# Softmax denominators by additions in SBUF, and fewer, larger stack DMAs

## The reference, cut to what matters

```python
Q = x @ W_Q.T; K = x @ W_K.T; V = x @ W_V.T          # 16 heads of 32
attn = einsum('bhqd,bhkd->bhqk', Q, K) * scale        # causal: keys after the query are masked
probs = softmax(attn, axis=-1)
y = einsum('bhqk,bhkd->bhqd', probs, V) @ W_O.T
x = layernorm(x + y)
x = layernorm(x + ffn(x))                             # top-1 of 8 experts, weighted
```

## Time and profile before

| | |
|---|---|
| median of 3 runs | 2947.55 us (2947.26 to 2957.64) |
| profiled execution, span from first to last instruction | 2947.9 us |
| TensorE, VectorE, ScalarE, GpSimd busy | 90%, 53%, 36%, 22% |

### The profile page before, as it was taken

One profiled execution on the slowest core, in us unless ns is written; L12 is line 12 of the kernel. 1 busy time (PEld: TensorE's weight loads), 2 busy tenths in 40 slices (PEclk: granted clock), 3 DMA queues, 4 the chain that ended last, 5 costly groups with the idle time before them and its releaser, 6 DMA issues. The chain is left out here.

```text
span 2947.9 us, 51268 instructions
## 1 busy us (share of the span) xinstructions
PE 2664.0 (90%) x16384; PEld 1627.8 (55%) x16385; DVE 1563.5 (53%) x2843; ACT 1065.4 (36%) x2153; POOL 660.7 (22%) x1022
## 2 busy tenths in 40 slices
PE   3999989998999999998999899989999999438886
PEld 2654665457554755475546654565447554436665
DVE  2566446645564456535663466445644564365554
ACT  2245314541445134522453145414541345132332
POOL 2111221113121311122112211131213110235544
PEclk9999999999999999999999999999999999669999
DMA  8422142314331433124221422152314320163332
GB/s 284 115 73 98 39 142 70 90 58 127 90 101 48 118 102 97 50 79 129 74 93 51 139 71 80 58 144 73 101 51 122 87 80 8 43 208 119 121 123 82
DMA packets 131006, 282.95 MB, mean 96 GB/s; under 512 B 33026, under 2 KB 42242, under 8 KB 128452
## 3 DMA queue, kind: packets, MB, share of 16 engines
q1 hardware_dynamic: 100920, 208.62, 23.7%
q0 software_dynamic: 28304, 70.64, 7.8%
q10 hardware_dynamic: 1536, 0.53, 0.1%
HBM read 133.04 MB, written 47.53 MB: 61 GB/s over the span
## 5 line engine op out<-in xcount | busy, mean ns | idle before, releaser
L638 ACT ACTIVATE probs<-score 128x512 f32<-128x512 f32 (+3 forms) x1536 | 690.2, 489 | 812.3 <-PE score L944 511.3
L695 DVE TENSOR_REDUCE tile_max<-maxp 128x1 f32<-128x512 f32 (+3 forms) x1072 | 679.7, 659 | 513.2 <-PE maxp L929 347.6
L940 PE MATMUL score<-q_stack,k_stack 97*128 97x512 f32 (+2 forms) x1536 | 548.5, 410 | 17.6 <-ACT probs L638 16.3
L880 PE MATMUL proj<-xt,w_qk 128*128 128x512 f32 x1536 | 458.8, 413 | 61.5 <-DMA w_qk<-w_qk_parts 49.8
L924 PE MATMUL maxp<-k_stack,q_stack 96*128 96x512 f32 (+2 forms) x1360 | 466.5, 397 | 16.2 <-DVE tile_max L695 12.5
L924 PEld LDWEIGHTS maxp<-k_stack,q_stack 96*128 96x128 f32 x1360 | 240.5, 193 | 312.3 <-issue 225.7
L940 PEld LDWEIGHTS score<-q_stack,k_stack 97*128 97x128 f32 x1536 | 290.3, 194 | 195.0 <-ACT probs L638 178.6
L880 PEld LDWEIGHTS proj<-xt,w_qk 128*128 128x128 f32 x1536 | 280.9, 193 | 118.5 <-DMA w_qk<-w_qk_parts 49.5
L962 PE MATMUL y_ps<-probs,v 128*32 128x512 f32 (+3 forms) x3072 | 327.5, 498 | 8.8 <-DVE rows L719 7.8
L962 PE MATMUL den_ps<-probs,ones_f 128*32 128x512 f32 (+3 forms) x3072 | 326.5, 497 | 0.0
L377 POOL DMA_DIRECT2D q_stack<-parts x256 | 126.6, 503 | 545.3 <-DVE parts L682 543.3
(11 more groups left out here) (138 smaller groups left out, 2312.0 us busy)
## 6 DMA issues: line engine op xcount, KB each, us to landing
w_qk<-w_qk_parts SPq DMA_DIRECT2D x64, 512.0 KB, 3.7
q_stack<-w_vo_parts SPq DMA_DIRECT2D x16, 2048.0 KB, 8.0
q_stack<-parts SPq DMA_DIRECT2D x512, 64.0 KB
k_stack<-parts SPq DMA_DIRECT2D x512, 64.0 KB
got<-dispatched SPq DMA_DIRECT2D x75, 257.0 KB
xt_raw<-x_t SPq DMA_DIRECT2D x32, 512.0 KB, 4.4
q_stack<-parts POOLq DMA_DIRECT2D x256, 64.0 KB, 2.3
k_stack<-parts POOLq DMA_DIRECT2D x256, 64.0 KB, 2.3
```

The costliest lines, as they stand in the source:

```text
L638: nc.scalar.activation(probs[:, 4 * (n % 2) + h, c:BANK], score[h % 2][:, c:BANK], ACT.Exp, scale=SCALE).then_inc(exp_done.sem, 1)
L695: nc.vector.tensor_reduce(tile_max[:, j, heads[0]:heads[-1] + 1, qb], tiles, AX.X, ALU.max)\
L880: mm = nc.tensor.matmul(proj[bank][:, :], w_qk[:, o, ws, k, :], xt[:, xs, k, t * BANK:(t + 1) * BANK], start=c == 0, stop=c == 3 * KT - 1)
L940: mm = nc.tensor.matmul(score[h % 2][:, c0:BANK], k_st[u % SETS][0:3 * DH + 1, h, kb * P:(kb + 1) * P], q_st[u % SETS][0:3 * DH + 1, h, t ...
```

## The change

Denominators are no longer summed by TensorE over key blocks. A new tensor `key_sum` holds, for four heads, 512 query columns. GpSimd copies the first key block's `probs` into it and adds each further block (`add_up`); TensorE multiplies only the finished sum with the ones, once a half (`denominators`). In unit 3 GpSimd takes heads 0 and 1, and VectorE heads 2 and 3. ScalarE, before it overwrites a slot of `probs`, now also waits for the additions of it. The sum's product is placed after group 0 (for the half before) and group 4 (for the first half), the last one after output 3 in the closing. Copies of sums are in groups 1 and 5, divisions of the half before in groups 2 to 5 (unit 3: group 2), those of unit 3's first half in group 6, outputs in groups 9 to 11.

The stack DMAs are issued by SP alone, one for all four heads of a block, 3 for a tile instead of 12. For this the host lays out the columns of W_Q and W_K with the head innermost, so that the 128 partitions of a part run in the same order as the 32 partitions by 4 heads of a stack. The scratch for descriptors of GpSimd's DMAs is set to 8192.

```diff
+        key_sum = sb("key_sum", [P, 4, BANK])
...
+        def send_tile(sp, b, u, o, t):
+            wait_job(sp, b, proj_free, ("p", u, 2 * o + t))
...
+            for block_row, part in enumerate(((HI, HI, LO), (HI, LO, HI))[o]):
+                sp.dma_start(dst[DH * block_row:DH * (block_row + 1), :, t * BANK:(t + 1) * BANK].bitcast(F32),
+                             parts[:, t, part, :].bitcast(F32)).then_inc(stack_in[t].sem, 16)
+
+        def add_up(eng, ops, b, u, j, heads, done, held):
+            t, kb = SCORE_GROUPS[j]
+            n = GROUPS * u + j
+            c, slot = column(kb, t), 4 * (n % 2)
+            new = probs[:, slot + heads.start:slot + heads.stop, c:BANK]
+            old = key_sum[:, heads, c:BANK]
+            if kb == 0:
+                eng.wait_ge(den_done.sem, den_done.at(b, HALVES * u + t))
+                hold(eng, held)
+                eng.wait_ge(exp_done.sem, exp_done.at(b, 4 * (n + 1)))
+                hold(eng, held)
+                ops.tensor_copy(old, new).then_inc(done.sem, 1)
+            else:
+                eng.wait_ge(done.sem, done.at(b, n if done is added else j))
+                hold(eng, held)
+                eng.wait_ge(exp_done.sem, exp_done.at(b, 4 * (n + 1)))
+                ops.tensor_tensor(old, old, new, ALU.add).then_inc(done.sem, 1)
...
 (GpSimd)
+                for u in range(UNITS):
+                    heads = slice(0, 4 if u < UNITS - 1 else 2)
+                    for j in range(GROUPS):
+                        add_up(pool, nc.gpsimd, b, u, j, heads, added, held_pool)
+                        if u == 2 and j in (2, 4, 6, 8) and not last:
+                            split_low(j // 2 - 1, xt_high.at(b, j // 2))
+                        if u == UNITS - 1:
+                            for tb in HIGH_GROUP.get(j, ()):
+                                low_y(tb)
...
 (ScalarE)
-                        if u and j == 0:
+                        if u and j == DEN_GROUP[1] + 1:
                             copy_sums(2 * u - 1)
...
                         if n >= 2:
                             weighed(act, b, n - 1)
+                            act.wait_ge(added.sem, added.at(b, n - 1))
+                            if u == UNITS - 1 and j >= 2:
+                                act.wait_ge(added_too.sem, added_too.at(b, j - 1))
...
-                        if j == HALF0:
+                        if j == DEN_GROUP[0] + 1:
                             copy_sums(2 * u)
...
 (VectorE)
                         if j == HALF0 + 1:
                             copy_y(2 * u)
-                            if u == UNITS - 1:
-                                divide(2 * u)
+                        if u == UNITS - 1:
+                            add_up(dve, nc.vector, b, u, j, slice(2, 4), added_too, held_dve)
+                        if u == UNITS - 1 and j == DEN_GROUP[0] + 2:
+                            divide(2 * u)
...
-                        if u == UNITS - 1 and j == 1:
+                        if u == UNITS - 1 and j == 2:
                             divide(2 * u - 1)
...
 (TensorE)
+                def denominators(n):
+                    adds = GROUPS * (n // HALVES) + (HALF0 if n % HALVES == 0 else GROUPS)
+                    pe.wait_ge(sums_copied.sem, sums_copied.at(b, n))
+                    if n >= HALVES * (UNITS - 1):
+                        pe.wait_ge(added_too.sem, added_too.at(b, HALF0 if n % HALVES == 0 else GROUPS))
+                    pe.wait_ge(added.sem, added.at(b, adds))
+                    for h in range(4):
+                        mm = nc.tensor.matmul(den_ps[DH * h:DH * (h + 1), :], ones_f[:, :], key_sum[:, h, :],
+                                              start=True, stop=True, tile_position=(0, DH * h))
+                    mm.then_inc(den_done.sem, 1)
...
-                    weigh(u, GROUPS - 1, False)
-                    weigh(u, GROUPS - 1, True)
+                    weigh(u, GROUPS - 1)
...
                     if name[0] == "o":
                         output(name[1])
+                        if name[1] == QUARTER - 1:
+                            denominators(2 * UNITS - 1)
```

More of the change, by code:

```diff
@@ L328, in stacked @@
         def stacked(eng, b, slot, tiles):
-            for s, gain in ((sp_in[slot], SP_GAIN), (pool_in[slot], POOL_GAIN)):
-                eng.wait_ge(s.sem, s.early(tiles * gain) if b is None else s.at(b, tiles * gain))
+            s, count = stack_in[slot], tiles * STACK_GAIN
+            eng.wait_ge(s.sem, s.early(count) if b is None else s.at(b, count))
         def max_bank(u, i):
@@ L539, in one_pass @@
                             .then_inc(rstd_ready.sem, 1)
-                if not last:
-                    send(b, 0)
                 pool.wait_ge(dest_ready.sem, dest_ready.at(b, 1))
@@ L1030, in one_pass @@
                         tile = [(lambda h=h: score_tile(u, j, h), 1) for h in range(4)]
-                        if j:
-                            sums, products = [[(lambda sums_too=s: weigh(u, j - 1, sums_too), 4)] for s in (True, False)]
-                        else:
-                            sums, products = [], []
-                        work = work[0:1] + tile[0:2] + products + tile[2:3] + work[1:2] + tile[3:4] + sums
+                        products = [(lambda: weigh(u, j - 1), 4)] if j else []
+                        work = work[0:1] + tile[0:2] + products + tile[2:3] + work[1:2] + tile[3:4]
                         total, passed, laid = sum(w for _, w in work), 0, 0
@@ L1048, in one_pass @@
                             pe.wait_ge(dest_ready.sem, dest_ready.at(b, 0))
+                        if u and j == DEN_GROUP[1]:
+                            denominators(2 * u - 1)
+                        if j == DEN_GROUP[0]:
+                            denominators(2 * u)
                         if u == UNITS - 1 and j in O_GROUP:
```

80 lines of the change are left out of this document (29 added, 51 removed).

## The result

The changed kernel takes 3255.6 us (median of four runs, 3253.6 to 3260.0); the kernel before took 2952.6 us beside it. The ratio is 1.103, interval 1.101 to 1.105. The forecast was 2998 us with a range up to 3055: the direction was right, the size was six times too small and outside the range.

The account below looks back on a forecast made before the run. It took TensorE at full clock as the bound. A batch: -6.7 - 3.6 + 3.7 + 7.7 + 3.9 + 1.0 = +6.0 us; times 8 and +3 gave 2999, stated as 2998 us, range 2890 to 3055.

Parts of the forecast that it names:

- rival 3: Slower: in ScalarE's unit 3 wait TensorE idles, its clock halves, +2 to +3.4 us a batch; 3050 us, 12%.
- The walk of GpSimd's turns: Units 0 to 2: exponentials of group n wait for the addition of n-2, 4.76 us a full group on GpSimd.
- Denominator matmuls gone, -237 us net: TensorE, all units: removed products save 9.4 us a unit, two sum products come back, net -7.4 us a unit.
- DMAs, 0: Stack DMAs merged and issued by SP: no TensorE wait ends on them, 0, bound 0 to -2 us a batch.
- Clock, 0: TensorE taken at its full 2.4 GHz clock; the sum has no term for time at 1.2 GHz.
- GpSimd's additions, 4.76 us: GpSimd's addition of four heads at 512 columns, scaled in proportion from a row of 128x1024 at 2384 ns.
- Unit 0 (-6.7): First unit of a batch: TensorE alone 8.4 us less, GpSimd's turns end 1.7 us over, so -6.7 us.
- unit 1 (-3.6): Second unit: -7.4 us of products, +3.8 for GpSimd's additions from group 4 on, so -3.6 us.
- Unit 2, +3.7: Third unit: additions and four subtractions on GpSimd end 11.1 us over TensorE's time; -7.4 + 11.1 = +3.7 us.
- Unit 3, +7.7: Fourth unit: GpSimd and VectorE additions go one after the other and divisions come late, output 3 at 52.3 instead of 44.6 us.
- Closing, +3.9: Batch end: the last sum behind output 3 delays divisions and values(1) by 2.86 and 1.00 us, +3.9 us.
- VectorE held, +0.5 us a unit: Units 1 and 2: multiplications that begin under a GpSimd addition are held, +0.5 us a unit, bounds 0 and 4.

Follow-up runs that it names:

- experiment 13: Kernel before without the denominator products of key blocks after the first, nothing in their place: 2789.4 us, ratio 0.9555.
- experiment 1: Kernel before with the merged stack DMAs alone, issued by SP, denominators still on TensorE: 3004.9 us, ratio 1.019.
- 14: Kernel before with merged stack DMAs and without the denominator products of key blocks after the first: 2948.6 us, ratio 0.999.
- 3: Changed kernel with every V product issued twice on a halved V, 300 us more of TensorE work: 3379.7 us, ratio 1.148.
- 12: Changed kernel with score products of heads 0 and 2 issued twice in units 2 and 3: 3270.0 us, ratio 1.109.
- experiment 8: Kernel before with five more VectorE reciprocals once a batch, ahead of the maxima of unit 2, group 7: 2966.4 us, ratio 1.019.
- 15: Changed kernel without GpSimd's and VectorE's additions and their waits, denominator products reading a constant: 2984.7 us, ratio 1.010.
- 16: Changed kernel with GpSimd's full-size additions into a spare tile, nobody waiting, VectorE's additions left out: 3049.8 us, ratio 1.034.

## Why the prediction was wrong, step by step

The chain of runs adds the parts of the change one after the other: products removed 0.956; merged DMAs 0.999; products grouped and divisions moved 1.010; GpSimd's additions unread 1.034; read and waited for 1.103. In us of 2950: -131, +127, +33, +71, +203. The first number is of the second kind, and each part is priced behind those ahead of it: the merged DMAs alone cost 55 us, and the 71 are a lower bound, so that the 203, which hold VectorE's additions too, are an upper one.

Two steps of the prediction failed: the DMAs, which it put at nothing, and the clock, which its sum left at nothing and its rival 3 priced at one short stretch a batch. The walk of GpSimd's turns, its main mechanism, was right in kind: the exponentials wait 85.4 us for its additions.

- **Denominator matmuls gone, -237 us net.** Wrong by almost half: 130 by experiment 13. The step took TensorE as the bound at every place because it was busy in 188 of 191 us. A row of busy time doesn't say how soon the next engine is behind it.
- **DMAs, 0.** The costliest step after the clock: 55 us alone, 127 with the products removed. The bound ("no wait ends on it") was read for the stacks only. What comes late beside the merged ones is others: the loop's end, w_qk (7.5 for 3.7 us), the negated maxima. One thing came earlier and wasn't foretold either: TensorE's wait for the first rows of the experts is 44.8 us for 54.3, and 44.6 in experiment 1.
- **Clock, 0, and in rival 3 only +2 to +3.4 us a batch.** This is the step that failed most. It lost 323 us of work in all, 40 us a batch in the first seven. The rival had the mechanism and priced one stretch of 3.4 to 6.8 us a batch; the trace has 67 in its first 82%, some nine a batch, up to 44.4 us long.
- **GpSimd's additions, 4.76 us.** 4.57 measured. The prediction cited a page's figure of 4497 ns (the Trainium skill, "GPSIMD Engine Reference", section "Elementwise — side-by-side cycle accounting") and went by its row; the page was nearer. It mattered little. In unit 2 the additions follow each other or a subtraction from group 7 on, as foretold, and group 11 begins 41.9 us after group 4 (1366.87 - 1324.94; 36.3 foretold).
- **Unit 0 (-6.7) and unit 1 (-3.6).** +0.1 and +0.3. There the walk had no DMAs, no held row maxima and no clock.
- **Unit 2, +3.7.** +15.0, with 31 us at half clock: -7.4 of products, +7.8 of idle time and 14.6 of work at a clock of 0.76.
- **Unit 3, +7.7.** +14.6. The order of events was right: the sum of group 4 waits for VectorE's addition 3 (a wait of 2.23 us), the copies of y wait 3.97 us for the multiplication, group 8 starts at 39.6 us (34.7 foretold), two-head additions read 3.40 us on GpSimd behind 1.23 on VectorE (3.6 foretold, but for VectorE's). The sum is -7.4 of products, +7.2 of idle time and 14.8 of work at a clock of 0.71. Moving the divisions back gave 27 us only.
- **Closing, +3.9.** values(1) waits 5.1 us (1.8 before), foretold 4 to 5; the rest of the 13 us is put down to the merged DMAs' gap of 8.5 us and the clock; this sum wasn't taken apart.
- **VectorE held, +0.5 us a unit.** The 256 multiplications take 156 us more (938 for 328 ns) and the 32 small copies 74 (2491 for 171 ns on average). The copy wasn't on the list, though TensorE waits for it. Removing the first brought 88 us (50 by ratio), removing the second nothing: the waits pass to the next late thing.

What stays open: why half clock lasts 13.7 to 44.4 us in the changed kernel, at much the same places in each batch, with TensorE busy in 80 to 98% of the longest ones, 10.2 or 13.7 behind a wait of 2.1 us in 14, and 0 to 10.2 behind the gaps made by hand. Neither the gap's length, nor three in a row, nor the denominator products behind it explain it; added work on TensorE shortens it (3, 12). So that the clock took 323 us is shown, and that waits of about 2 us can start it; which waits of the changed kernel start its long stretches is not.

## What to carry to other kernels

When work is taken off a full engine, price first what the next engines allow, by a run or a row in which they are late, and then the clock: in experiment 8 a gap of 2.3 us cost 5.1, in others more of the clock or nothing of it, so a range belongs in the sum, and not zero. GpSimd's additions here held VectorE's copies and multiplications between SBUF tensors, down to 16 columns; list those that TensorE waits for and place the additions where there are none. Merging DMAs saves issues, and here small transfers, a weight load and the work at the loop's end came later for it.

## What the runs showed of the hardware that was not expected

- Adding work to TensorE in the changed kernel raised its clock: 300 us of products cost 124, 72 us cost 14. Taking products off alone left it as it was (0.968, experiment 13).
- A VectorE copy of 128x16 took up to 4.2 us under one GpSimd addition; reciprocals (0.94 us) and reductions (0.69 us from PSUM, 0.17 of 16 columns from SBUF) were not held.
- A DMA of 256 KB between SBUF tiles took some 4.5 us with the queue to itself; four of 64 KB, issued by GpSimd, land in 2.3 us each.
- The time at half clock isn't set by the idle time alone. In the first 82% of the span, without the first wait of 50 us for weights, idle and half-clock us were 97 and 85 (before), 136 and 67 (13), 206 and 331 (14), 237 and 307 (15), 246 and 427 (16), 297 and 478 (3), 316 and 771 (after), 342 and 580 (12). From 136 to 316 us of idle time it grows some four times as much as this, but three pairs of neighbours in this list go the other way (before and 13, 14 and 15, after and 12).
